# A conditional batch transform ahead of a routed low-rank layer: the 16 weight tables kept in on-chip memory and picked by GpSimd, low parts taken straight from PSUM, and a reordered load queue

## The reference, cut to what matters

```python
# x: (64, 64, 1024) f32; itok: (64,) int32 in 0..15; cond_weights: (16, 64, 64)
W = cond_weights[itok]                        # one 64x64 table for each of the 64 batches
y = einsum('bct,bcd->bdt', x, W)
base = einsum('bsi,oi->bso', y, W_org)        # W_org: (1024, 1024)
q = einsum('bi,ki->bk', y.mean(axis=1), Wq)
coeffs = softmax(einsum('bk,ek->be', q, lora_keys) / sqrt(128))
h = einsum('bsi,eir->bser', y, lora_down)     # 8 experts, rank 64
delta = einsum('be,bser,ero->bso', coeffs, h, lora_up)
return x + base + delta
```

## Time and profile before

| | us |
|---|---|
| median of 3 runs | 719.81 |
| the profiled execution, its own time | 721.46 |
| its span, first to last instruction | 719.4 |
| TensorE busy | 708.5 |
| VectorE (DVE) busy | 498.3 |
| ScalarE (ACT) busy | 242.0 |
| GpSimd (POOL) busy | 119.0 |

### The profile page before, as it was taken

The page is one execution under the profiler, slowest core; times in us unless marked ns, Lnnn a source line. Parts: engine busy times, 40 slices in busy tenths (PEclk is TensorE's granted clock), DMA queues, the critical chain, the costliest instruction groups (busy, mean ns, idle before and its releaser), DMA issues.

```text
span 719.4 us, 10708 instructions
## 1 busy us (share of the span) xinstructions
PE 708.5 (98%) x3409; PEld 595.2 (83%) x3409; DVE 498.3 (69%) x813; ACT 242.0 (34%) x468; POOL 119.0 (17%) x108
## 2 busy tenths in 40 slices
PE   7989999999999999999999999999999999999997
PEld 7878888888888888888888878888888888888876
DVE  4978767475575674674756898676777777687774
ACT  4447244254352362442533832211222222121220
POOL 2200000000000000000000023333233332333350
PEclk9999999999999999999999999999999999999999
DMA  8986583772763753532452746667777676666732
GB/s 237 287 253 212 162 244 145 201 216 104 234 212 133 217 172 116 169 118 59 140 183 103 272 163 185 220 221 228 234 234 235 220 234 219 221 208 216 271 123 88
DMA packets 100986, 138.61 MB, mean 193 GB/s; under 512 B 18874, under 2 KB 70082, under 8 KB 98114
## 3 DMA queue, kind: packets, MB, share of 16 engines
q1 hardware_dynamic: 100592, 137.85, 59.8%
q10 hardware_dynamic: 338, 0.07, 0.0%
HBM read 82.32 MB, written 55.57 MB: 192 GB/s over the span
## 4 chain that ended last, share of the span: by engine, by line
PE 92%; DVE 3%; issue 2%; DMA 2%; SPq 0%; ACT 0%; POOL 0%; DVEq 0%; POOLq 0%
PE x_ps L1446 22%; PE w_ps L1446 17%; PE x_ps L1383 12%; PE x_ps L1349 12%; PE h_ps L1349 11%; PE w_ps L1383 9%; PE y_ps L1308 7%; DMA x_sb<-in_x_dram 1%; PE w_ps L1434 1%; DVE tb_l L858 1%; DVE blk L861 1%; DMA cw_sb<-in_L_cond_weights_dram 0%; DVE ba_l L858 0%; PE w_ps L1308 0%; DVE down_l L858 0%
## 5 line engine op out<-in xcount | busy, mean ns | idle before, releaser
L557 POOL TENSOR_TENSOR blk<-blk,blkx 128x512 f32<-128x512 f32 x60 | 93.8, 1565 | 275.6 <-DVE blk L861 203.1
L861 DVE TENSOR_TENSOR blk<-w_ps,blk 128x512 f32<-128x512 f32 x96 | 66.1, 688 | 67.6 <-PE w_ps L1383 32.3
L1446 PE MATMUL x_ps<-tb_h,ba_h 128*128 128x512 f32 x256 | 100.0, 391 | 0.8 <-DVE ba_l L858 0.4
L1446 PE MATMUL x_ps<-tb_l,ba_h 128*128 128x512 f32 x256 | 99.6, 389 | 0.0
L1446 PE MATMUL x_ps<-tb_h,ba_l 128*128 128x512 f32 x256 | 99.6, 389 | 0.0
L593 ACT ACTIVATE ba_h<-bs 128x512 fp32r<-128x512 f32 x64 | 38.1, 626 | 122.9 <-DVE bs L858 122.9
L1446 PE MATMUL w_ps<-tb_h,ba_h 128*128 128x512 f32 x192 | 74.9, 390 | 0.0
L1446 PE MATMUL w_ps<-tb_h,ba_l 128*128 128x512 f32 x192 | 74.7, 389 | 0.0
L1446 PE MATMUL w_ps<-tb_l,ba_h 128*128 128x512 f32 x192 | 74.7, 389 | 0.0
L861 DVE TENSOR_TENSOR blk<-x_ps,blk 128x512 f32<-128x512 f32 x64 | 42.5, 682 | 32.3 <-PE x_ps L1446 32.3
L874 DVE TENSOR_REDUCE ysum<-y_full 128x8 f32<-128x512 f32 x64 | 41.5, 680 | 32.8 <-ACT y_full L593 32.8
(11 more groups left out here) (103 smaller groups left out, 1389.7 us busy)
## 6 DMA issues: line engine op xcount, KB each, us to landing
x_sb<-in_x_dram SPq DMA_DIRECT2D x32, 512.0 KB, 4.4
y_dram<-y_full SPq DMA_DIRECT2D x64, 256.0 KB, 3.1
yb<-y_dram SPq DMA_DIRECT2D x32, 512.0 KB, 7.5
out_dram<-blk SPq DMA_DIRECT2D x64, 256.0 KB, 3.9
blkx<-in_x_dram SPq DMA_DIRECT2D x30, 512.0 KB, 7.1
r_dram<-blk SPq DMA_DIRECT2D x56, 256.0 KB, 2.4
blk<-r_dram SPq DMA_DIRECT2D x14, 1024.0 KB, 6.7
t_dram<-st SPq DMA_DIRECT2D x16, 448.0 KB, 4.2
```

The lines of the kernel that those rows point to most:

```text
L557: pool.tensor_tensor(blk[p % 3][:, b, :], blk[p % 3][:, b, :], blkx[:, h, n, :], ALU.add).then_inc(x_added, 1)
L861: nc.vector.tensor_tensor(dst, a, b, ALU.add).then_inc(done, 1)
L1446: mm = nc.tensor.matmul(bank, ba[s][n][:, k, :], tb[w][n][:, k, :], start=(first and k == 0 and i == 0), stop=(k == 3 and i == 2), skip_gr ...
```

## The change

- A DMA from ACT's queue loads all 16 tables at once: 64 partitions by 16 rows of 256 bytes, 256 KB. The loads of one table each, on SP and ACT, are gone (64 DMAs of 16 KB, with their register loads).
- GpSimd's `turn_cw` loads the two numbers of a tile into registers, and copies each table from an address taken from the register into its half of `cws`: two copies of 64 partitions by 64 elements in place of one of 128 by 128. Each copy waits until the one before has completed. The zeros around the tables are now written once, into `cws`.
- `yg` moves to space shared with `gs`; five waits are added ahead of its write, on things that DVE itself has waited for or made by then.
- SP asks for x of the first four tiles at once; the stores of halves 2 and 3 come ahead of the first up pieces, and x of tile 6 ahead of the last two up pieces and of the stores of halves 4 to 7 (in the kernel before it stands behind all of them); x of tile 7 stands between the stores.
- DVE makes the low parts of halves 0, 2, 4 and 6 from PSUM directly, and the copies to `y_full` of 2, 4 and 6 come after it, around the first pieces of the down weights.
- TensorE makes half 5 of y behind the third pass of L1344 and no longer between the first and the second.

```diff
-        cw_sb = small("cw_sb", [P, 4, BT, C])
+        table = small("table", [C, NCOND, C])
         cws = small("cws", [P, 3, BT, 2, C // 2])
...
-            load_x(0)
-            load_x(1)
-            sp.wait_ge(cond_loaded, 16)
-            sp.wait_ge(first_steps, 1)
-
-            row_0 = row(0)
-            row_1 = row(1)
-            load_row(0, row_0)
-            load_x(2)
...
-            load_row(3, row_3)
+            for t in range(4):
+                load_x(t)
             load_down_half(0, 0, down_loaded[0])
             load_down_half(1, 0, down_loaded[1])
             load_down_half(0, 1, down_rest_loaded)
             load_down_half(1, 1, down_rest_loaded)
             sp.dma_start(wq_raw[:, :], wq).then_inc(wq_loaded, 16)
             load_x(4)
-            load_cw(4)
             store_y(0)
             store_y(1)
             load_down(2)
             load_down(3)
             load_x(5)
-            load_cw(5)
+            store_y(2)
+            store_y(3)
             load_up(0)
             load_up(1)
-            store_y(2)
-            store_y(3)
+            load_x(6)
             load_up(2)
             load_up(3)
-            for n in range(4, 8):
-                store_y(n)
-            for t in (6, 7):
-                load_x(t)
-                load_cw(t)
+            store_y(4)
+            store_y(5)
+            load_x(7)
+            store_y(6)
+            store_y(7)
...
             def turn_cw(t):
 
-                i = t % 4
-                pool.wait_ge(cw_loaded[i], 16 * BT * (t // 4 + 1))
+                rows = [pool.value_load(cond_sb[0:1, BT * t + b:BT * t + b + 1], min_val=0, max_val=NCOND - 1)
+                        for b in range(BT)]
                 if t >= 3:
                     pool.wait_ge(y_done, tile_made(t - 3))
-                pool.tensor_copy(cws[:, t % 3, :, :, :],
-                                 cw_sb[:, i, :, :].rearrange("p b (d h) -> p b h d", h=2)).then_inc(cw_ready, 1)
+                for b in range(BT):
+
+                    pool.wait_ge(cw_ready, BT * t + b)
+                    pool.tensor_copy(cws[b * C:(b + 1) * C, t % 3, b:b + 1, :, :],
+                                     table[:, :, :].rearrange("c n (d h) -> c n h d", h=2)[:, bass.ds(rows[b], 1), :, :]
+                                     ).then_inc(cw_ready, 1)
...
-            pool.memset(cw_sb[:, :, :, :], 0.0).then_inc(first_steps, 1)
+            pool.memset(cws[:, :, :, :, :], 0.0).then_inc(first_steps, 1)
...
+            pool.wait_ge(first_steps, 4)
+            pool.wait_ge(cond_loaded, 16)
+            pool.wait_ge(table_loaded, 16)
             turn_cw(0)
             turn_cw(1)
             turn_cw(2)
             turn_cw(3)
+            pool.wait_ge(cw_ready, BT * 4)
             for t in range(3):
                 split_y(t)
+            pool.wait_ge(y_lo[1], 3)
             turn_cw(4)
+            pool.wait_ge(cw_ready, BT * 5)
             split_y(3)
+            pool.wait_ge(y_lo[1], 4)
             turn_cw(5)
...
             act.dma_start(cond_sb[:, :], cond_v).then_inc(cond_loaded, 16)
+            act.dma_start(table[:, :, :], table_v).then_inc(table_loaded, 16)
             act.dma_start(keys_sb[:, :], lora_keys).then_inc(keys_loaded, 16)
...
                 dve.wait_ge(y_hi[r], t + 1)
                 if n in BY_DVE:
-                    dve.wait_ge(*copied(n))
+
+                    sub(yq[1][:, 0:4, i * P:(i + 1) * P], y_bank(n).rearrange("p (k n) -> p k n", k=4),
+                        yq[0][:, 0:4, i * P:(i + 1) * P], y_lo[0])
+                    return
...
+            split_y(0)
             copy_y(0)
-            split_y(0)
-            copy_y(2)
             split_y(2)
-            copy_y(4)
             split_y(4)
-            copy_y(6)
             split_y(6)
             split_down_half(0, 0)
+            copy_y(2)
             split_down_half(1, 0)
+            copy_y(4)
+            copy_y(6)
...
                         for i, (s, w) in enumerate(PASSES):
                             if i == 1:
-                                make_y(5)
                                 pe.wait_ge(y_lo[0], 4)
...
+                        make_y(5)
                         continue
```

More of the change, by code:

```diff
@@ L63, in adaln_ffn @@
     cond_v = cond.rearrange("(a b) -> a b", a=1)
+    table_v = cond_w.rearrange("n c d -> c n d")
     down_v = lora_down.rearrange("(n a) (k p) r -> n p (a k) r", n=DP, k=KC)
@@ L133, in adaln_ffn @@
         ysum = small("ysum", [P, KC, BQ])
-        yg = small("yg", [P, BQ, E, KC])
+        yg = at("yg", 178176, [P, BQ, E, KC])
         z = small("z", [P, BQ * E])
@@ L158, in adaln_ffn @@
         x_loaded = [sem(f"x_loaded_{i}") for i in range(4)]
-        cw_loaded = [sem(f"cw_loaded_{i}") for i in range(4)]
+        table_loaded = sem("table_loaded")
         down_loaded = [sem(f"down_loaded_{n}") for n in range(DP)]
@@ L317, in load_x @@
                 sp.dma_start(x_sb[:, i, :], x_v[t, :, :]).then_inc(x_loaded[i], 16)
-            def load_cw(t, batches=range(BT)):
-                i = t % 4
[L321 to L325, removed]
             def load_down(n):
@@ L390, in store_out @@
                 sp.dma_start(out_rows[pair(p), h][:, n * N:(n + 1) * N], blk[p % 3][:, b, :]).then_inc(out_stored[p % 3], 16)
[L392 to L396, removed]
             def load_down_half(n, r, done):
@@ L451, in _ @@
                         load_x(t + 4 + m)
-                        load_cw(t + 4 + m)
                     if 1 <= q <= 4 and m % 2 == 0:
@@ L593, in copy @@
                 nc.scalar.activation(dst, src, ACT.Copy).then_inc(done, 1)
[L595 to L599, removed]
             def copy_y(n):
@@ L707, in _ @@
             copy(sexp[:, 0, :], ident[:, 0:E], act_ready)
[L708 to L716, removed]
             split_y(0)
@@ L901, in gate_sums @@
                 dve.wait_ge(y_summed, 8 * q + 8)
+                if q >= 1:
+                    for n in (P5, P6):
+                        dve.wait_ge(ga_hi[n], 2 * q)
+                        dve.wait_ge(ga_lo[n], 2 * q)
+                    dve.wait_ge(s_ready[3], 2 * q)
                 nc.vector.tensor_tensor(yg[:, :, :, :],
@@ L1300, in make_y @@
                 pe.wait_ge(x_loaded[i], 16 * (t // 4 + 1))
-                pe.wait_ge(cw_ready, t + 1)
+                pe.wait_ge(cw_ready, BT * (t + 1))
                 if n in BEFORE:
```

## The result

The changed kernel has a median of 727.96 us over 6 runs (726.09 to 729.02), the kernel before 719.78 us over 6 runs of the same job (718.87 to 722.74): ratio 1.0096, 95% interval 1.0068 to 1.0125. The medians differ by 8.2 us, and the ratio, formed over the runs, stands for 6.9 us (4.9 to 9.0). The kernel became slower; I had forecast 717.7 with a range up to 721.5.

A forecast was written before the change was run, and what follows sets the result against it. TensorE, busy 708.5 of 719.4 us, bounds the kernel, so its first 60 us decide. Head +0.8, group (0,0) and tile 4 -0.9, x of tile 6 -1.95 sum to -2.05: 717.7 us, range 714.8 to 721.5.

The forecast's parts named there:

- the head: Kernel start to the first h product: table and GpSimd's register loads make it 0.8 us later, 15.55.
- group (0,0): First h group on TensorE: three passes back to back, then half 5; 6.45 us from first h product, 1.2 less.
- tile 4's table: GpSimd's turn for tile 4, behind three subtractions, ends later than TensorE wants it: 0.3 us lost.
- x of tile 6: TensorE's stall at 39.7 us goes; TensorE alone gains 4.2 us, of which 1.95 counted.
- signs of being wrong: Tile 3's table ready before 11 or after 15 us, or TensorE's first-phase up products without gaps.
- the landing of the table: Kernel start: the 256 KB table, issued beside x, lands at 6.0 us; other cases 4.6 and 9.2.
- the case of 4.6: Landing time in us of the table if only one load of x is served ahead of it.
- Fewer DMAs on SP: SP's queue: 64 issues with register loads go; x and down pieces come 2 to 3 us sooner; gain zero.
- Rival 2: Table waits for all four loads of x: head +4.0 us, time 721.0; chance 0.19, shared with 0.6 us register loads.
- What the registers cost: GpSimd's turn: two register loads 1.14 us, 1.75 per tile with copies; tiles 0 to 3 ready 8.0 to 13.2.
- Rival 3: GpSimd's register loads cost far more than SP's, 1081 ns each: sum +4.35 us, 724.2; chance 0.12.
- late next: After tile 6's stall goes, DVE and ACT limit TensorE: 2.25 us return as waits between 52 and 60 us.

The follow-up runs named there:

- a_hold: The changed kernel, with x of tiles 1 to 3 and everything behind it on SP held until the table has landed: 720.52 us, ratio 1.0004 to the kernel before.
- a_tfirst: The changed kernel, with the load of all tables issued first in SP's queue and not by ACT: 719.22 us, ratio 0.9989 to the kernel before.
- a_warm: The changed kernel, with 44 unused products on zeros at TensorE's start in place of 12: 725.66 us, ratio 1.0066 to the kernel before.
- a_turn4: The changed kernel, with GpSimd picking tile 4's table ahead of its subtractions of the low parts: 725.21 us, ratio 1.0079 to the kernel before.
- a_all: The changed kernel, with table first on SP, tile 4's table before the subtractions, eight register loads ahead of the table wait: 717.25 us, ratio 0.9964.
- a_best: As a_all on the changed kernel, but only the four register loads of tiles 0 and 1 ahead of the table wait: 716.42 us, ratio 0.9948.
- a_less: a_best with DVE's four differences of the up weights cut to 8 of 512 columns, output not the reference's: 714.07 us in one run.
- b_x6: The kernel before, with only SP's order changed, x of tile 6 ahead of two up pieces and four stores: 719.92 us, ratio 0.9998.
- b_psum: The kernel before, with only the low parts from PSUM, the later copies and the later half 5: 720.38 us, ratio 1.0002.
- b_both: The kernel before, with the edits of b_x6 and b_psum and none of the table's: 719.43 us, ratio 0.9999.

## Why the prediction was wrong

Against the sum of the prediction, on the pair of profiles: the head was forecast at +0.8 and measured +7.46, group (0,0) at -1.2 and -1.23, tile 4's table at +0.3 and +2.43, x of tile 6 at -1.95 and -1.99. One of the signs of being wrong came true: tile 3's table was ready at 18.44, and I had named "after 15".

**The step that failed: the landing of the table.** I had it at 6.0, "since ACT issues it in the time of SP's second load", with 9.2 as the upper bound for a table behind all four loads of x. It was 11.2. 11.2 - 6.0 is 5.2 of the 6.7 us by which H was later than forecast (22.21 against 15.55). Three things were wrong in it.

First, I took the table for something that is served as a whole at one place among the loads of x. Two thirds of its rows did move by 6.0 us, as if it stood behind two of the loads; the last third moved in small portions until 10.2.

Second, the sum that gave 4.6, 6.2 and 9.2 (2.0, the loads of x ahead, 1.2) is about 1 us short even without the down weights. a_hold is the case of 4.6, one load of x beside the table, and it landed at 5.6; a_tfirst, with nothing ahead, would be 3.2 by this sum and was 4.8. The last row had moved 0.6 to 1.4 us before each landing, and no term stood for that.

Third, the part "Fewer DMAs on SP" was put at zero. I had seen that x and the down weights come sooner, and asked only who would use them, not what they would delay. With the waits for registers gone from SP's queue the down weights are issued from 2.80 us on and not from 8.72, after and before:

```profile
2.80 9.27 SPq L389 DMA_DIRECT2D down_raw<-in_L_ffn_lora_down_dram  x8
```
```profile
8.72 4.43 SPq L400 DMA_DIRECT2D down_raw<-in_L_ffn_lora_down_dram  x8
```

a_tfirst and a_hold show that what SP has in flight is the cause as a whole: the same 256 KB land 4.0 to 4.3 us after their issue when all or most of it comes behind them. With the missing 1 us the bound of 9.2 becomes 10.2; that the last 1.0 up to 11.2 is the down weights fits the packets, but no run shows it by itself. Rival 2 of the prediction was this case, at too small a size; the trace bears out what it took from the Trainium skill ("DMA: Bandwidth & Descriptors", section "Queues, rings and completion order"), that engines take turns between queues, in so far as the rows of ACT's queue moved between those of SP's for 6 us.

**The second: the low clock.** I had left TensorE's clock out of the head. It was idle from 6.1 to 13.6 us but for one small product, and the clock fell to half. The halves of y then ran slower than the tables came. From GpSimd's last copy to H I had forecast 2.36 us; it was 3.77, and 2.53 in a_warm at full clock. So the clock is 1.2 us of H, and another 1.6 behind half 8. With the landing (5.2) and the 0.2 by which a_warm exceeds my 2.36, the miss of H is accounted for to 0.1 us. In a_turn4, with the same idle time ahead, the stretch took 2.91, so this price changes from one execution to the next.

**What the registers cost: right.** I had 1.75 us per tile and tile 3 ready 7.2 after the table. It was 1.64, and 7.24 (11.20 to 18.44). GpSimd's eight register loads in the head take 288 ns at the median (283 to 503), as SP's do in the earlier trace rows. Over the whole kernel:

```profile
L512 POOLq TENSOR_LOAD <-cond_sb x64: 283/534/1244, 11.3 to 309.1; - x64
```

The median over the whole kernel is 534 ns and one took 1244, so GpSimd's loads are slower later on; no wait of TensorE for a table follows there. Rival 3 fell with that. The floor of about 600 ns that the Trainium skill gives ("DMA: Bandwidth & Descriptors", section "Latency and other measured facts") does not hold here: two loads, their steps and two copies together take 1.64 us. But these 7.2 us were on the path, where a tile of before needed one copy of 0.3 behind its loads: a_all and a_best gain because they take all or half of these first loads out from behind the table.

**Group (0,0): right.** 6.45 forecast, 6.45 measured, against 7.68.

**Tile 4's table: mechanism right, size wrong.** GpSimd's turn came late, as I wrote, and half 8 waited 0.69 us for it; but the low clock came behind it, and the whole was 2.43 and not 0.3. a_turn4 took 2.3 of it away.

**x of tile 6: right against the profile, wrong against the kernel.** In the pair of profiles the gain from the scores to U is 1.99, against 1.95 forecast, with three new waits at the up products ended by ACT (62.19, 65.67 and 67.67), behind DVE. Together with smaller gaps they make the way from the scores to U 2.1 us longer than in a_less, against the 2.25 that I had said would come back. So what I had asked for as "late next" was there, and a_less, made on a_best, shows that it is DVE. That both numbers agree is in part luck of the execution: the profiled one of before was 2 us longer than the two that I took later, and in those U - H is 43.9 to 44.0 already, so that the stall costs 0.1 us there. b_x6 shows it: U - H 43.89, no gain in the median. I had noted that this execution took 1.65 us more than the median, and then booked as a gain of the median what about one execution in four loses.

**The sum of the two.** b_psum and b_both have the same U - H (43.39 and 43.36). Both edits shorten TensorE's way to a point where, by what a_less shows, it waits for DVE. Against an execution without the low clock the two and the early table of tile 4 are worth 0.9 us together (44.0 to 43.1), where I had booked 2.85 for the two less the lateness of that table.

## What to carry to other kernels

One large load beside others is there when its last row is, and at the head of a kernel its turn among the queues is worth more than its bytes: put what everything waits for first in the queue, and hold back what is not needed yet. Before booking a stall as a gain, set the profiled execution's own time against the median; if it is late by as much as the stall costs, the stall may be what made it late. Another profile of the same kernel tells whether the stall is always there, and the clocks and spans of the executions that were only timed tell how often. Where two engines are nearly level, take the distance between two marks in each variant: if a second edit adds nothing to what the first gives, another engine may hold the distance, and cutting that engine's work shows whether it does.

## What the runs showed of the hardware that I had not expected

TensorE's granted clock did not fall behind the same idle time each time. The windows of the kernel after at 11 and 32 us:

```profile
11.00:13.00 2.00, 0.24 (x1) 0.18 (x1) 0.17 (x1) 0.00 (x0) 0.17 (x1) 0.50 1.36 218
...
32.00:34.00 2.00, 1.92 (x12) 1.95 (x13) 1.97 (x4) 0.00 (x0) 1.27 (x1) 0.68 1.00 410
```

The first follows 5 us without work (the clock is at 0.71 from 8 to 10 us and at 0.50 from 9 to 11). The second follows the gate product (16 small matmuls of 8 columns in 1.85 us) and 0.69 us without work. In a_warm and a_tfirst the same product is followed by 0.68 and 0.69 us without work, and the clock stays at full (2.4 GHz, not 1.2). The stall for x of tile 6 was followed by the low clock when it was 2.24 us long and not when it was 1.47 or 1.66; but in the head of b_x6 2.46 us without work, waiting for a table, were not followed by it (granted clock 1.00 from 12 to 16 us). So the length of the gap alone does not tell whether the clock falls, and what else decides stays open here.
